# Cross-attention and expert layer in one kernel: shift rows issued by SyncE between the stack copies, low parts on VectorE, first biases as products

## What is computed

```python
Q = proj(q, Wq, bq); K = proj(k, Wk, bk); V = proj(v, Wv, bv)
scores = jnp.einsum('bhid,bhjd->bhij', Q, K) / math.sqrt(DH)
scores = scores + _alibi_bias(L, scores.dtype)[None]
attn = jax.nn.softmax(scores, axis=-1)
x = jnp.einsum('bhij,bhjd->bhid', attn, V)
...
shared = jax.nn.silu(xf @ Sg) * (xf @ Su) @ Sd
probs = jax.nn.softmax(xf @ Wr, axis=-1)
topk_p, topk_i = jax.lax.top_k(probs, K)
...
y = jax.nn.silu(xf @ wg) * (xf @ wu) @ wd
```

## Time and profile before

| | us |
|---|---|
| median of 3 runs | 248.33 |
| lowest, highest | 248.07, 248.94 |
| the profiled execution | 249.56 |
| its span, first to last instruction | 247.8 |
| mean granted clock of TensorE | 0.979 of full |

### The profile page before, as it was taken

One profiled execution on the slowest core, in us unless ns is written; L12 is line 12 of the kernel. 1 busy time (PEld: TensorE's weight loads), 2 busy tenths in 40 slices (PEclk: granted clock), 3 DMA queues, 4 the chain that ended last, 5 costly groups with the idle time before them and its releaser, 6 DMA issues.

```text
span 247.8 us, 6092 instructions
## 1 busy us (share of the span) xinstructions
PE 216.5 (87%) x1937; PEld 177.5 (72%) x1937; DVE 172.4 (70%) x600; ACT 124.9 (50%) x298; POOL 83.4 (34%) x192
## 2 busy tenths in 40 slices
PE   2978588878989698989999899979997989989995
PEld 2666346666779577967798688957895779768985
DVE  4689614796789556993698478856885589654882
ACT  8475543656454545356446534655545424644320
POOL 2501012501483118610791059114830182018100
PEclk9999957999999999999999999999999999999999
DMA  5553582163303460156106510734044500170000
GB/s 152 169 90 118 107 296 79 36 105 101 75 3 98 69 173 0 42 105 162 31 3 138 144 48 1 136 91 105 3 116 90 132 1 4 26 171 0 0 25 21
DMA packets 13079, 20.24 MB, mean 82 GB/s; under 512 B 2800, under 2 KB 9440, under 8 KB 12544
## 3 DMA queue, kind: packets, MB, share of 16 engines
q1 hardware_dynamic: 12080, 18.64, 31.3%
q10 hardware_dynamic: 976, 1.32, 1.9%
HBM read 16.03 MB, written 3.78 MB: 80 GB/s over the span
## 4 chain that ended last, share of the span: by engine, by line
PE 35%; issue 32%; POOL 13%; DMA 7%; DVE 6%; ACT 5%; ACTq 0%; POOLq 0%; SPq 0%; DVEq 0%
PE ps_up L501 7%; POOL hid L1315 6%; PE ps_m L527 6%; DMA stacks_sb<-nmT 6%; PE ps_pv L434 4%; PE ps_up L506 3%; PE ps_pv L441 2%; PE ps_st L415 2%; DVE nmax L966 2%; PE ps_s L360 2%; DVE stacks_sb L1195 1%; DMA ident<-in_c_ident 1%; POOL qk_parts L1308 1%; PE ps_st L469 1%; PE ps_m L456 1%
## 5 line engine op out<-in xcount | busy, mean ns | idle before, releaser
L730 ACT ACTIVATE probs<-ps_st 128x512 f32<-128x512 f32 x64 | 37.8, 594 | 27.4 <-PE ps_st L415 27.2
L786 ACT ACTIVATE th<-ps_up 128x256 f32<-128x256 f32 x72 | 27.6, 383 | 35.6 <-PE ps_up L506 35.4
L527 PE MATMUL ps_m<-wd_sb,hid 128*128 128x128 f32 x288 | 44.2, 281 | 0.0
L1070 DVE SCALAR_TENSOR_TENSOR tg<-th,ps_up 128x256 f32<-128x256 f32 x72 | 29.8, 414 | 20.2 <-ACT th L786 19.7
L966 DVE TENSOR_REDUCE nmax<-ps_s 128x4 f32<-128x512 f32 x64 | 41.9, 679 | 0.5 <-issue 0.4
L1315 POOL TENSOR_TENSOR hid<-hid,crep 128x256 f32<-128x256 f32 x56 | 39.0, 729 | 5.2 <-ACT x2n L760 3.4
L527 PEld LDWEIGHTS ps_m<-wd_sb,hid 128*128 128x128 f32 x288 | 37.7, 191 | 0.6
L415 PE MATMUL ps_st<-stacks_sb 98*128 98x128 f16 x256 | 25.7, 225 | 9.5 <-DMA stacks_sb<-nmT 6.7
L1076 DVE TENSOR_TENSOR hid<-tg,ps_up 128x256 f32<-128x256 f32 x72 | 29.7, 412 | 1.0
L1271 POOL TENSOR_TENSOR ve<-mv,eps_sb 128x1 f32<-128x1 f32 x16 | 3.0, 189 | 79.6 <-DVE mv L1017 79.6
L415 PEld LDWEIGHTS ps_st<-stacks_sb 98*128 98x128 f16 x256 | 17.9, 100 | 15.6 <-DVE ps_st L985 6.3
(11 more groups left out here) (149 smaller groups left out, 447.4 us busy)
## 6 DMA issues: line engine op xcount, KB each, us to landing
crep<-cw_dram SPq DMA_DIRECT2D x28, 256.0 KB, 4.4
stacks_sb<-qk_dram SPq DMA_DIRECT2D x32, 128.0 KB, 4.0
...
```

The lines of the kernel that those rows point to most:

```text
L527: last = mm(ps_dn[:, b * P:(b + 1) * P], hid[:, buf, c, b * P:(b + 1) * P], wd_sb[:, c, :], start=(c == 0 and b == 0), stop=(c == SHARED), ...
L730: fn(probs[:, b, g * HG * P:(g + 1) * HG * P], ps_st[(g + 1) % 2][:], ACT.Exp).then_inc(exp_sb, 1)
L786: fn(th[:, c % 2, :], ps_up[c % 2][:, 0, :], ACT.Tanh, scale=0.5).then_inc(tanh_sb, 1)
L1070: v.scalar_tensor_tensor(out=tg[:, c % 2, :], in0=th[:, c % 2, :], scalar=1.0, in1=ps_up[c % 2][:, 0, :], op0=ALU.add, op1=ALU.mult).then_ ...
```

## The change

- The DMA of the shift rows moves from ScalarE's queue to SyncE's. `stacks` is cut in three, `write_parts`, `stack_k` and `stack_q`. For a step the order on SyncE is: writes, shift of b = 0, stack_k, shift of b = 1, stack_q; for group 0 the shift of b = 0 comes ahead of the writes.
- The low parts of q and k are made by VectorE for every group, in one instruction from the bank. `qk_copy` on ScalarE, `qk_full` and GpSimd's `qk_low` go.
- Group 0 has no seeds: its biases are products, and its banks are numbered the other way round (`scores_bank`), so that its first tile does not wait for the bank in which the projections of group 1 lie.
- TensorE's order: `late_down(2)` before `up(f, 0)`, `scores_T(a, 0, 1)` before `shift_T(a, 1)`, `scores_T(a, 1, 2)` before `values_T(a, 0)`; for group 0 `scores_T(0, 0, 0, 0)` before `shift_T(0, 1)`, and one `keep_clock(2)` goes.
- The memsets of `select` and `cwT_r` move from VectorE to GpSimd, and GpSimd no longer waits for `x2n_sb` before it weights experts.

```diff
-            def stacks(p, buf):
+            def write_parts(p, buf):
...
+            def stack_k(p, buf):
...
+            def stack_q(p, buf):
...
+            def shift_rows(a, b, buf):
+                sp.wait_ge(nm_sb, 2 * a + b + 1)
+                sp.dma_start(qs[buf][ZROWS:AROWS, :, b * P:(b + 1) * P], nmT[:, b, :]).then_inc(s_nm[b], 16)
...
             def step(f, a, p, q, abuf):
-                if p is not None:
-                    stacks(p, 1 - abuf)
-                if a is not None and at_start(a): load_more()
+                if at_start(a): shift_rows(a, 0, abuf)
+                if p is not None: write_parts(p, 1 - abuf)
+                if not at_start(a): shift_rows(a, 0, abuf)
+                if p is not None: stack_k(p, 1 - abuf)
+                shift_rows(a, 1, abuf)
+                if p is not None: stack_q(p, 1 - abuf)
+                if at_start(a): load_more()
...
-                bank, n, seeded = ps_st[(g + 1) % 2], 2 * NHG * a + NHG * b + g, (b, g) in ((0, 0), (1, 0), (1, 1))
+                bank, n = scores_bank(a, g), 2 * NHG * a + NHG * b + g
+                seeded = not at_start(a) and (b, g) in ((0, 0), (1, 0), (1, 1))
...
+                if at_start(a) and (b, g) == (0, 1):
+                    pe.wait_ge(qklo_sb, 4)
...
+                scores_T(0, 0, 0, 0)
                 shift_T(0, 1)
-                keep_clock(2)
-                scores_T(0, 0, 0, 0)
...
+                late_down(2)
                 up(f, 0)
-                late_down(2)
...
+                scores_T(a, 0, 1, abuf, f=f)
                 shift_T(a, 1)
-                scores_T(a, 0, 1, abuf, f=f)
...
+                scores_T(a, 1, 2, abuf)
                 values_T(a, 0)
-                scores_T(a, 1, 2, abuf)
...
-            def qk_low_first(k):
-                dve.wait_ge(qkhi_sb, 2 - k)
-                bank = ps_k0 if k else ps_qk[:, 0:T]
+            def qk_low(p, k):
...
+                bank = ps_k0 if k and at_start(p) else ps_qk[:, k * T:(k + 1) * T]
...
+                if p is not None: qk_low(p, 1)
                 row_max(a, 1, 0)
+                if p is not None: qk_low(p, 0)
                 gate(f, 1)
...
-                    pool.wait_ge(x2n_sb, NB * f + NB)
```

82 lines of the change are left out of this document (33 added, 49 removed).

## The result

| | before | after |
|---|---|---|
| median of 4 runs, us | 248.20 | 241.25 |
| lowest, highest | 247.50, 248.94 | 240.88, 241.43 |
| profiled execution, its span | 249.56, 247.8 | 241.20, 239.4 |
| mean granted clock in it | 0.979 | 0.986 |

The ratio is 0.9718, with a 95% interval from 0.9687 to 0.9749. The forecast was 246.1 us with a range from 243.0 to 249.8: the sign was right, the size was too small by 4.9 us. The two traces lie 8.4 us apart and the medians 7.0, because the trace of before was one of its slower executions.

The account below looks back on a forecast made before the run. TensorE was taken as nearly the bound, its idle time as what can be won. First group +2.7, first step +0.3, middle steps -4.5, last step -0.7 give -2.2 us: 246.1 us on the median, range 243.0 to 249.8.

Parts of the forecast that it names:

- the middle steps: The five steps f = 1 to 5: 0.9 us faster each, 4.5 us together.
- the first group: Opening group: later second shift costs 1.4 us, bias products at half clock 1.3 us; 2.7 us slower.
- f = 0: First full step: first shift behind the writes lands 0.6 us later, less a part of (f); 0.3 us slower.
- (a): Middle steps, TensorE: late_down(2) goes into the 0.41 us gap ahead of up(f,0); by itself worth nothing.
- (b): Middle steps, VectorE: two products' low parts add 0.8 us, of which gaps before the gates swallow 0.77.
- (c): Middle steps: ScalarE loses two copies and two issues, GpSimd two low parts; ScalarE's saving priced at nothing.
- (d): Middle steps, SyncE: first shift behind three writes lands after 2.7 us; new wait before scores_T(a,0,0), 0.6 us taken.
- (e): Middle steps: second shift, issued ahead of stack_q, lands before it is wanted; the 1.05 us wait before scores_T(a,1,0) goes.
- (f): Steps, TensorE: scores_T(a,1,2) ahead of values_T(a,0) fills the 0.39 us gap; 0.37 us taken.
- The clean win: Rival: shifts land in 2.0 us, no wait before scores_T(a,0,0); 5.0 us faster, 243.3 us, chance 0.20.
- The hostage: Rival: first shift behind the writes on SyncE lands late, scores_T(a,0,0) stands 1.5 us; 250.8 us, chance 0.17.
- VectorE was not the bound: Rival that VectorE is the bound: its added 0.8 us a step are not swallowed; 249.2 us, chance 0.15.

Follow-up runs that it names:

- e3_down_only: Kernel after with late_down(2) put back behind up(f,0): 241.25 us (0.973).
- e3_shift_only: Kernel after with shift_T(a,1) put back ahead of scores_T(a,0,1): 242.96 us (0.9803).
- e2b_gpsimd_low: Kernel after with the steps' low parts made by ScalarE and GpSimd again and the first shift issued ahead of the writes: 239.67 us (0.9709).
- e8_wait_x2n: Kernel after with GpSimd's wait for both halves of x2n before weighting hidden chunks put back: 240.90 us (0.9702).
- e3_tensor_order: Kernel after with all three of TensorE's moves in the steps undone (late_down(2), shift_T(a,1), values_T(a,0)): 245.87 us (0.996).
- e7: Kernel before, unaltered, traced once more: 248.60 us (1.0041).
- e5: Kernel after with the first group's seeds put back in place of its bias products: 243.33 us (0.984).
- e2_hostage: Kernel after with the steps' low parts made by ScalarE and GpSimd again, the first shift still behind the writes: 244.92 us (0.9871).

## Why the prediction was wrong, step by step

The forecast was 2.2 us faster; between the two traces it was 8.4. Of the 6.2 us in between, 3.0 are in the middle steps (7.5 for 4.5), 2.5 in the first group (a loss of 0.2 for 2.7), 0.9 in f = 0, and the last step gave 0.2 less. Three terms failed: how long TensorE's clock stays low in the first group, the landing time of a free shift, and the move of shift_T, which stood at nothing.

**What bounds the kernel.** Right: TensorE, and what was won was its idle time.

**(a) late_down(2).** Right: worth nothing by itself (e3_down_only, 0.1 us).

**(b) VectorE's 0.8 us.** Right in the chain that I followed: the seeds end 12.8 us after x_hi's first product instead of 12.6. Wrong in one place: I looked for its delay at weights_T. It falls on shift_T(a,1), which waits for VectorE's split maxima, and the move that I booked only as a delay of the second shift avoids just that. 0.3 us a step, 1.5 us in all, stood at nothing in my sum (e3_shift_only).

**(c) ScalarE, GpSimd and the wait for x2n.** Right (e2b_gpsimd_low, e8_wait_x2n).

**(d) The first shift behind the writes.** The step that failed first in the order of the text. It was issued 5.2 us after x_hi's first product (100.16 less 95.00) where I had 4.8 (102.35 less 97.59), so I had its place. But I gave it 2.7 us to land, near the upper end of 2.0 to 3.0, because one gap between last packet and product measured 1.7 us (by the single packets it is 1.9: the last ended at 108.82). The 1.5 us to the last packet were right. The 1.2 us of arrival that I set behind it are 0.4 to 0.6 for a free shift; the 1.7 came from one that landed among the reads. Free it is 2.01 to 2.22 in all. By 2.7 TensorE would have stood 0.6 us at 102.28; it stood 0.1. Nor did it lose in f = 0, where I had booked 0.3 us: the wait there is 0.28 instead of 1.22 us.

**(e) The wait before scores_T(a,1,0).** It went, as forecast, and doubly: the reads are earlier (except in f = 2, where the k reads go out 7.85 us after x_hi's first product, 7.70 in the kernel before), and the shift is ahead of half of them. I had 0.55 us a step for (d) and (e) together; the steps of before less those of e3_tensor_order give 1.43, 0.42, 0.38, 0.38 and 0.87, 0.7 as a mean. By the second trace of before (e7), whose middle steps but f = 3 are shorter, less is left: 0.92, 0.33, 0.21 and 0.44 us for f = 1, 2, 4 and 5. I had priced all five by f = 2. The waits of before were 1.55, 1.05, 0.66, 1.01 and 1.25 us, and f = 1 and f = 5, with the longest, gained most.

**(f) values_T.** Right in mechanism, 0.37 taken, 0.44 to 0.51 measured, and 0.90 in f = 1.

**The first group.** The landing was right (30.96 for 31.6), and the price up to values_T too: 35.34 less 33.37 is 2.0 us for 2.7 in the sum. Then I wrote that I saw no reason for TensorE to be spared, and took the end of the half level from the trace of before. It ended 3 us sooner, and the second half of the values products (38.32) took 1.07 us at the full level where they had taken 1.93 (at 36.41 in the kernel before). With the 0.7 us less before it this is the largest single miss, 2.5 us. With bias products instead of seeds TensorE had no pause from 31 to 37 us. With the seeds back (e5) the half level lasted 10.2 us again in the trace. The first group lost 0.2 us instead of 2.7. That TensorE's gapless run is what ends it sooner is inferred: in ten traces of kernels with the first group of after the half level lasted 6.8 us nine times and 3.4 once; with seeds (before twice, e5) it was 10.2 us three times. No run varied the pauses alone, and the length is not fixed by the kernel: by their mean clocks 2 of 6 executions of e5 and 14 of 68 of the kernel before lost about as little to the clock as the kernel after.

**The rivals.** The clean win was the case that came, and it is what I had at 243.3 us with a chance of 0.20; the 2 us that it lacks are shift_T's, f = 0 and the first group's clock. The hostage is real, and only the earlier writes keep it away (e2_hostage: 3.6 us above the kernel after and 5.2 above the run with the shift ahead of the writes). VectorE was not the bound.

**The sum.** Of the 8.4 us between the traces TensorE's moves give 5.1 (e3_tensor_order), the first group -0.2, and the 3.5 that are left are put down to the shift's landing, for which no run stands alone. By the medians it is 4.6 of 7.0 for TensorE's moves and 2.4 for all the rest. In the five middle steps the moves and the rest are 4.0 and 3.5, where I had 1.85 (0.37 for values_T, nothing for shift_T) and 2.75; the last full step's 0.7 was 0.5, since the gap of late_down(2) gives nothing there either; f = 0 and the first group, booked as losses of 0.3 and 2.7, are a gain of 0.6 and a loss of 0.2.
